# A two-layer transformer on one core: layer 0's attention probabilities scaled, turned by VectorE's blocks and DMA, and multiplied in plain fp32

## What is computed

```python
q = jnp.einsum('btd,ndh->btnh', x, q_kernel)      # 16 heads of 128
kv = jnp.einsum('bsd,ckdh->cbskh', x, kv_kernel)  # 8 shared key/value heads
q, k = apply_rope(rms_norm(q)), apply_rope(rms_norm(k))
logits = jnp.einsum('btkgh,bskh->bkgts', qg * ATTN_SCALE, k)
logits = jnp.where(mask, logits, finfo.min)       # causal, window 128
probs = jax.nn.softmax(logits, axis=-1)
enc = jnp.einsum('bkgts,bskh->btkgh', probs, v)
out = jnp.einsum('btnh,nhd->btd', enc, out_kernel)
```

## Times and the profile before

| | us |
|---|---|
| median of 3 runs | 687.75 |
| lowest, highest | 686.14, 690.43 |
| the profiled execution, its own time | 687.28 |
| the span of its trace | 685.4 |

### The profile page before, as it was taken

One profiled execution on the slowest core, in us unless ns is written; L12 is line 12 of the kernel. 1 busy time (PEld: TensorE's weight loads), 2 busy tenths in 40 slices (PEclk: granted clock), 3 DMA queues, 4 the chain that ended last, 5 costly groups with the idle time before them and its releaser, 6 DMA issues.

```text
span 685.4 us, 16439 instructions
## 1 busy us (share of the span) xinstructions
PE 671.9 (98%) x4369; PEld 603.4 (88%) x4369; DVE 575.1 (84%) x1755; ACT 441.4 (64%) x1741; POOL 362.5 (53%) x555
## 2 busy tenths in 40 slices
PE   7999999999999998999999999999999999999998
PEld 3789999999999997888888899999999999978887
DVE  6979999899899999887875898989898988796333
ACT  4888888888798886431436666666666666764222
POOL 5998888898889873200138963415142324027000
PEclk9999999999999999999999999999999999999999
DMA  6010210101020001100024657465656555100000
GB/s 245 2 48 2 108 48 2 47 0 46 1 108 31 31 8 71 47 0 1 16 91 91 143 123 174 105 148 123 140 119 148 127 125 136 32 1 1 1 31 32
DMA packets 127117, 47.23 MB, mean 69 GB/s; under 512 B 93520, under 2 KB 122064, under 8 KB 126928
## 3 DMA queue, kind: packets, MB, share of 16 engines
q1 hardware_dynamic: 103824, 34.49, 20.8%
q10 hardware_dynamic: 23232, 12.06, 5.9%
HBM read 34.28 MB, written 12.26 MB: 68 GB/s over the span
## 4 chain that ended last, share of the span: by engine, by line
PE 85%; DVE 6%; issue 3%; ACT 3%; DMA 2%; SPq 0%; POOL 0%; ACTq 0%; DVEq 0%; POOLq 0%
PE bank L528 12%; PE bank L958 12%; PE bank L415 11%; PE bank L520 11%; PE bank L547 6%; PE bank L383 5%; PE bank L449 5%; PE bank L455 4%; PE bank L376 4%; PE bank L1032 3%; PE bank L431 3%; PE bank L470 3%; PE bank L1036 3%; DVE x L713 1%; PE bank L1052 1%
## 5 line engine op out<-in xcount | busy, mean ns | idle before, releaser
L713 DVE SCALAR_TENSOR_TENSOR x<-bank,rinv,x 128x256 f32<-128x256 f32 x256 | 121.0, 473 | 3.3 <-PE bank L415 1.0
L691 ACT ACTIVATE probs<-scores,negmax 128x128 f32<-128x128 f32 (+1 forms) x256 | 117.8, 475 | 6.7 <-DVE negmax L760 5.8
L600 ACT CAST enc_hi<-bank 128x256 fp32r<-128x256 f32 x128 | 47.8, 374 | 75.1 <-PE bank L455 68.8
L843 POOL TENSOR_TENSOR a_hi<-raw_a,zero 128x384 fp32r<-128x384 f32 (+1 forms) x60 | 44.2, 737 | 70.8 <-PE bank L547 70.8
L315 POOL TENSOR_TENSOR ln_r<-ln_ve,neg_half 128x1 f32<-128x1 f32 x26 | 17.1, 656 | 117.3 <-DVE ln_ve L289 117.3
L724 DVE TENSOR_TENSOR enc_lo<-bank,enc_hi 128x256 fp32r<-128x256 f32 x128 | 53.9, 421 | 24.7 <-PE bank L383 16.0
L415 PE MATMUL bank<-b_hi,enc_hi 128*128 128x256 f32 x256 | 73.4, 287 | 0.5 <-DVE x L713 0.5
L415 PE MATMUL bank<-b_hi,enc_lo 128*128 128x256 f32 x256 | 72.1, 282 | 0.0
L415 PE MATMUL bank<-b_lo,enc_hi 128*128 128x256 f32 x256 | 71.7, 280 | 0.0
L861 POOL TENSOR_TENSOR rot_a<-rot_a,rot_b 128x384 f32<-128x384 f32 x64 | 64.8, 1012 | 8.4 <-DVE rot_b L831 7.2
L859 POOL TENSOR_TENSOR rms_r<-meansq,neg_half 128x3 f32<-128x3 f32 x64 | 54.9, 857 | 7.4 <-DVE negmax L760 2.2
(11 more groups left out here) (185 smaller groups left out, 2368.0 us busy)
## 6 DMA issues: line engine op xcount, KB each, us to landing
shuffle<-blocks ACTq DMA_DIRECT2D x57, 192.0 KB, 2.5
arrived<-shuffle SPq DMA_DIRECT2D x228, 48.0 KB, 2.2
raw_a<-in_wa SPq DMA_DIRECT2D x40, 192.0 KB, 3.1
raw_a<-in_wa SPq DMA_DIRECT2D x9, 512.0 KB, 4.3
raw_b<-in_wb SPq DMA_DIRECT2D x16, 256.0 KB, 2.8
hid_last<-in_wax SPq DMA_DIRECT2D x2, 512.0 KB, 5.2
w_a<-in_w2t SPq DMA_DIRECT2D x1, 1024.0 KB, 4.9
raw_b<-in_wdown SPq DMA_DIRECT2D x2, 512.0 KB, 3.3
```

The source lines that it names most:

```text
L600: nc.scalar.copy(enc[0][:, hh, b * D:(b + 1) * D], bank[O_BANK][:, 0:D]).then_inc(s["ehi"], 1)
L691: nc.scalar.activation(probs[:, c % 4, c0:c1], scores[:, c % 2, c0:c1], ACT.Exp, bias=negmax[:, c % 2, r:r + 1], scale=-1.0, accum_out=row ...
L713: nc.vector.scalar_tensor_tensor(out=x[:, m % 8, :], in0=output_bank(m)[:, hh * D:(hh + 1) * D], scalar=rinv[:, u, r:r + 1], in1=x[:, m % ...
```

## The change

For layer 0's units 0 to 55 (MOVED is now a pair, 56 for layer 0 and 57 for layer 1):

- the three TensorE transposes, ScalarE's two copies and VectorE's lo part of the probabilities go, and so do the split of the values (L623, L836) and the waits for them;
- VectorE makes the reciprocal of the row sums of each unit at the end of its slot (dve_norm); in the next slot ScalarE scales `probs` in place, 128 and 256 columns (act_scale), VectorE transposes in blocks ahead of its work on the scores (dve_blocks), and ScalarE issues the write to HBM after its copies and ahead of the exponentials (send_blocks); SyncE fetches in four transfers (fetch_turned), in a slot order of its own with layer 0's weight loads (sp_slot0);
- TensorE multiplies the values in plain fp32 straight from `arrived`, 256 columns and 128 columns;
- since the probabilities are already divided by their sums, the output product accumulates both heads in one 256-column bank region, and VectorE adds it to `x` once, with a plain addition; the even units up to 50 use PT_BANK for it, so the wait for the addition before is one unit looser;
- the loop begins at slot 9, not 11, so GpSimd makes the mean squares from unit 12 on, not 14 (FIRST_MEANS); `w2` and the down weights are loaded after SyncE's slots; a wait of ScalarE for a zeroed tile moves from the start to its first Silu.

```diff
-FIRST_SLOT, LOOP_FROM, LOOP_STEP, LOOPS, LAST_SLOT = -5, (11, 9), 16, 3, 70
+FIRST_SLOT, LOOP_FROM, LOOP_STEP, LOOPS, LAST_SLOT = -5, (9, 9), 16, 3, 70
...
+LAST_OUTPUT_PT = UNITS - 14
-MOVED = UNITS - 7
+MOVED = (UNITS - 8, UNITS - 7)
...
+            if L == 0 and m <= LAST_OUTPUT_PT and m % 2 == 0:
+                return bank[PT_BANK]
...
-                    need(pe, s["opadd"], it, m)
+                    need(pe, s["opadd"], it, m - 1 if L == 0 and m <= LAST_OUTPUT_PT + 1 else m)
+                one = normalized(L, it, m)
                 for h in range(2):
                     for i, (l, r) in enumerate(PASSES):
...
+                        cols = slice(0, D) if one else slice(h * D, (h + 1) * D)
+                        mm = pe.matmul(output_bank(L, m)[:, cols], enc[l][:, h, t * P:(t + 1) * P],
+                                       b_w[slot][r][:, h * D:(h + 1) * D], start=i == 0 and not (one and h),
+                                       stop=i == 2 and not (one and h == 0))
...
-                need(pe, s["ptev"], it, m + 1)
+                if normalized(L, it, m):
+                    need_turned(pe, L, it, m)
+                else:
+                    need(pe, s["ptev"], it, m + 1 - (MOVED[0] if L == 0 else 0))
...
+                    pe.matmul(bank[O_BANK][:, 0:256], v_plain(L, m // 8 % 2, 2 * b)[:, vc:vc + DH], there[:, 0:256],
...
+        def act_scale(act, it, m):
+
+            if live(it, m) and moved(0, it, m):
+                need(act, s_norm, it, m + 1)
+                nc.scalar.mul(probs[:, m % 4, 0:128], probs[:, m % 4, 0:128], rinv[:, m % 16, 0:1])
+                nc.scalar.mul(probs[:, m % 4, 128:384], probs[:, m % 4, 128:384], rinv[:, m % 16, 1:2]).then_inc(s_scaled, 1)
...
             if c <= TAIL_SLOT or L == 1:
                 act_encoded(act, L, it, c - 4)
+            if L == 0:
+                act_scale(act, it, c - 1)
...
-                    if t % 2 == 0 and (it is not None or m >= FIRST_SPLIT[0]):
-                        nc.scalar.copy(v_part(0, 0, m // 8 % 2, t // 2), bank[PJ_BANK + m % 2][:, 384:512])
...
+            if L == 0:
+                send_blocks(act, 0, it, c - 1)
...
+                if normalized(L, it, m):
+                    if hh == 0:
+                        need(dve, s["op"], it, m + 1)
+                        nc.vector.tensor_tensor(x[:, m % 8, :], output_bank(L, m)[:, 0:D], x[:, m % 8, :],
+                                                ALU.add).then_inc(s["opadd"], 1)
+                    return
...
+        def dve_norm(dve, it, c):
+
+            if live(it, c) and moved(0, it, c):
+                need(dve, at[0]["exp"], it, 2 * c + 2, 2)
+                nc.vector.reciprocal(rinv[:, c % 16, :], rowsum[:, c % 16, :]).then_inc(s_norm, 1)
...
                 dve_turned_lo(dve, L, it, c - 3)
+                if L == 0:
+                    dve_blocks(dve, 0, it, c - 1)
                 dve_scores_wait(dve, L, it, c)
...
+            if L == 0:
+                dve_norm(dve, it, c)
+            else:
+                dve_blocks(dve, 1, it, c)
...
+            def sp_slot0(c):
+
+                if c >= 1:
+                    fetch_turned(0, c - 1)
+                if c % 8 == 4 and c // 8 + 3 < PAIRS + 2:
+                    load_a(0, None, c // 8 + 3, 0)
+                if c % 8 == 7 and c // 8 + 2 < PAIRS:
+                    load_b(0, None, c // 8 + 2)
...
+            for c in range(MOVED[0] + 1):
+                sp_slot0(c)
+                if c == 20:
+                    load_late(0)
+            sp.dma_start(w2_a[:, :, :].rearrange("p a d -> p (a d)"), w2t).then_inc(s_w2, 16)
```

161 lines of the change are left out of this document (70 added, 91 removed).

## The result

The changed kernel takes 691.8 us in the median (687.88 to 698.51 over 20 runs), the kernel before 687.21 beside it. The ratio is 1.0071, with an interval of 1.0053 to 1.0088. So the change costs 4.6 us where I had forecast a gain of 11.5, and the time lies above the predicted range of 672 to 686. The step that failed is not TensorE's saving. It is "VectorE's part, hidden": I let the chain through ScalarE's scaling and VectorE's transpose pass beside the slot, and it is the slot, because it closes on itself. In layer 0's attention it costs 5.3 us of the 16.6 by which the forecast was missed there. The pauses at the loop's returns (6.6) and one late fetch (2.1), both priced near nothing, cost most of the rest.

A forecast was written before the change was run, and what follows sets the result against it. TensorE bounds the kernel (85% of the wait chain), with GpSimd next in layer 0: 12.0 us gained at most, less 0.5 at loop returns, 11.5. From 687.3 that gives 675.8, say 676, range 672 to 686.

The forecast's parts named there:

- VectorE's part, hidden: Layer 0 slots: VectorE's work about 3.45 us, hidden behind 3.73; chain over two slots about 6.8 against 7.46, not binding.
- TensorE saves 15.1 us, a slot of 3.65: Layer 0 attention: dropped transposes and plain fp32 value products save 12.5 plus 2.6 us of TensorE time.
- TensorE's full gain: Rival: GpSimd does not bind in layer 0, so TensorE's whole 15.1 us comes through, 672 us; chance 0.08.
- GpSimd decides, at 7.45 a pair: Layer 0: GpSimd's unchanged work, 3.73 us a slot, limits the gain to 12.0 us, however much TensorE saves.
- The loop's return, 0.5 us: Layer 0's two loop returns: ScalarE stands 2.2 us, delaying VectorE's rotary product to GpSimd; 0.5 us lost, range 0 to 2.4.
- ScalarE hidden at 3.4 a slot: Layer 0: copies swapped for scalings (0.4 to 0.8 us) plus the write's issue; 3.3 to 3.7 us busy, taken as 3.4.
- The round trip, hidden: Layer 0 blocks to HBM and back: 6.1 us against 8.1 available, 2.0 us of cover, so no cost.
- each load now stands after a fetch: SyncE's queue in layer 0: weight loads follow fetches, semaphores given slots earlier, so they were priced at nothing.
- The rival had seven units delayed by 1.5 us: Round trip ends last: 512 KB weights ahead of a fetch delay seven units, 697 us; round-trip rival's chance 0.07.
- GpSimd stopped by the transposes: Rival: GpSimd halts while VectorE transposes, slot up to 4.31 us, 20 us slower, 707; chance 0.04.
- The signs given: Trace signs for layer 0: if right, no L431 until unit 56; if wrong, exponentials starting late behind the write's issue.
- GpSimd idle ahead of L861 in every slot, which would mean that VectorE's chain sets the pace: Listed sign that the forecast is wrong: GpSimd waiting in every layer 0 slot; no size given.

The follow-up runs named there:

- experiment 11: Changed kernel with late load behind layer 0's slots, VectorE's cast ahead of the transpose, slots written out, queries' low part left out from unit 24: 674.37 us.
- experiment 6: Changed kernel with the late load behind layer 0's slots and ScalarE's two scalings left out (no division by the row sums): 676.4 us, ratio 0.983.
- experiments 3 to 5: Changed kernel with VectorE's cast ahead of the block transpose, 685.28 us; also late load behind layer 0's slots, 682.26; also its loop slots written out, 677.34.
- experiment 10: Kernel of experiment 5, with GpSimd's subtraction in the weight splitting on half the columns from layer 0's third weight group on: 677.36 us.
- experiment 5: Changed kernel with late load behind layer 0's slots, VectorE's cast ahead of the block transpose, and layer 0's 48 loop slots written out: 677.34 us.
- experiment 7: Changed kernel with layer 0's 48 loop slots written out for every engine, nothing else: 684.96 us, ratio 0.9958.
- second profile: Changed kernel, unedited, profiled once more: 691.35 us, where the execution profiled first took 697.09.
- experiment 8: Kernel before the change with layer 0's 48 loop slots written out for every engine: 686.25 us, ratio 0.9987.
- experiment 9: Kernel of experiment 7, with the late load's two 512 KB halves issued at slots 18 and 22 instead of both at slot 20: 680.62 us.
- experiment 1: Changed kernel with the two 512 KB of late columns loaded after SyncE's last slot of layer 0, not behind slot 20: 690.56 us.

## Why the prediction was wrong

- *TensorE saves 15.1 us, a slot of 3.65.* Right. The short slots of after have it, and in experiment 11 nearly all of the later ones. The time that I gave TensorE's full gain was 672; the kernel of experiment 11 takes 674.4.
- *VectorE's part, hidden: a chain of 6.8 against 7.46, "so it does not bind".* This step failed first. The chain's members were right: I counted 1.15 us from the reciprocal to the transpose, and it is 1.11. The error is what I took them for. I followed one unit through two slots. But VectorE's queue is in order, so the reciprocal of the next slot stands behind this slot's transpose and all that follows it, and the chain closes on itself in one slot: 1.11 + 2.94 = 4.05 in the long one, 3.63 in the short one, 7.69 a pair. My own numbers came near it: 3.45 of work a slot and, of the 1.15, some 0.6 of waiting make 4.05. (That it is 4.05 exactly is luck: the 3.45 is counted from a slot of before without the queries' low part, L772 there.) I had written it down as maxima that start 0.3 later, and looked for nothing that waits for them.
- *GpSimd decides, at 7.45 a pair.* Not in the changed kernel, since the ring is longer. As the next bound behind TensorE's it was right: without the scalings GpSimd sets the pair, at 7.48 (experiment 6). The 7.48 of experiments 3 to 5 is another one and near it by chance; there the ring through the low parts holds the pair, GpSimd's key scaling ends 1.3 to 1.5 us ahead of L483, and relieving GpSimd does nothing (experiment 10). The pace that I read the earlier trace rows holds a wait of 0.16 for GpSimd's own mean square. All looped kernels have it, none that is written out, and there GpSimd needs 7.39. "However much TensorE saves" was too strong by that, and by the lead that GpSimd can use up: experiment 11 has slots of 3.65 for 17 pairs.
- *The loop's return, 0.5 us.* Mis-sized: some 4.6 us in the changed kernel (experiments 5 and 7), 7.1 where the clock falls behind it (second profile), 1.1 in the one before (experiment 8). ScalarE's pause was in the rows, but I priced it through VectorE's rotary product and GpSimd. It comes through the scalings, which have no slack (experiment 6: 4.11 in place of 6.3 to 6.4 without them).
- *ScalarE hidden at 3.4 a slot.* Its busy time is as said: the two scalings take 0.31 + 0.40 from start to start, 0.71 of the 0.4 to 0.8 allowed. The amount was never the matter; the place of the scalings was.
- *The round trip, hidden, and "each load now stands after a fetch".* The steady trip is hidden. The sentence on SyncE's loads is false at slot 20, where three loads stand in a row: 2.0 to 4.7 us of wait, and 4.3 us of time where the load was split (experiment 9), 1.2 where it was moved away in the loop (experiment 1). I had counted the regular load of 512 KB there and overlooked the two halves of the late one. The rival had seven units delayed by 1.5 us; in after it is one, by more. A single load ahead of a fetch made one slot of 5.80 in experiment 5.
- *GpSimd stopped by the transposes.* Not seen. In experiment 11 its pair is 7.39 beside a transpose in each slot, no more than before.
- *The signs given.* No L431 until unit 56, and the exponentials not held up by the issue: both so. "GpSimd idle ahead of L861 in every slot, which would mean that VectorE's chain sets the pace" was listed as the sign of error, and it came. L892, as it is called in after, starts 0.93 to 0.95 us behind the instruction before it, and 0.82 to 0.84 in the back-to-back stretch of before. That is 0.1 us a slot, 0.2 a pair, which is 7.69 against 7.48, too small for the list of waits. The sign that told was the wait of one engine for another that waits for it.

## What to carry to other kernels

Where a change puts one engine's instruction between two of another engine's in the same slot, add up the ring: from the first through the other engine to the second, and on through the rest of the in-order queue to the first again. If that exceeds the slot, it is the slot, whatever the busy times say; and a pause of the engine in the middle is paid nearly in full (2.5 to 3.0 us of pause, slots 2.1 to 2.9 longer). Fill the gap with work that needs neither, but ask first what stands behind each moved instruction on both queues: one move gave 6.5 us back, a second one of the same kind cost 63. And look up every transfer that shares a queue with a new one, slot by slot, the ones that come only once too.

## What the runs showed of the hardware

- ScalarE's pause at the loop's return, with no releaser, is 2.0 to 2.2 us in before and 2.8 to 3.0 in after (2.5 to 3.0 in experiment 1). Two of them are 1.1 us of time in one kernel and some 4.6 in the other.
- The loop costs something in each pair as well, where an engine waits: GpSimd's pair is 7.48 in the loop and 7.39 written out, the ring's 7.69 and 7.60.
- TensorE's granted clock fell to 0.50, the lower of its two levels (1.2 of 2.4 GHz), behind a wait of 4.74 us (1.00 again from 121 us on), and behind waits of 1.87 and 1.80 at the two returns of the second profile. It stayed at 1.00 behind 2.01 in the same profile, behind 2.43 in experiment 7 and behind 1.95 and 1.82 in the second profile of experiment 1. So the length of one wait does not tell whether it falls. Where it falls, the wait is paid once more in part: 5.30, 4.55 and 4.49 for slots of 3.7.
- VectorE's subtraction with both inputs in SBUF (L754) took 2.55 us when it began within a GpSimd addition of 2.36, and up to 1.48 in the trace of before, where the median of its 56 is 0.42. The Trainium skill (SBUF — State Buffer, section Who interferes with whom) says that a VectorE instruction with two SBUF inputs contends with a GpSimd instruction that reads SBUF. By that rule the trace agrees, 2.55 beside 2.36. In the profile of experiment 6 it is 2.53, begun 0.11 us behind such an addition. In the second profile of after the subtraction began 0.52 ahead of the addition, and it took 0.85. No run moved the one away from the other by an edit.
- Executions of the changed kernel scatter by 10.6 us (687.88 to 698.51), those of before by 4.4. Late fetches, clock and the start of layer 1 are seen to vary between its two profiles. Its four executions with a mean granted clock of 1.000 took 687.88 to 693.61 us, the others up to 698.51. Which of them makes the 3 us between the profiled and the other executions of experiment 1 was not found.
